# TensorE's increments on a drain behind each group of matmuls, in the three edge stages of a graph network

## The reference

```python
h = relu(layernorm(x))
x = x + L0(h, src, dst)                 # attention pooling, one logit per source node
h = relu(layernorm(x))
x = x + L1(h, edge_index, edge_attr)    # two TransformerConvs, 8 heads and 1 head

def L0(N, W1, w2, src, dst):
    e = (tanh(N @ W1.T) @ w2)[src]
    ex = exp(e - segment_max(e, dst)[dst])
    return segment_sum((ex / segment_sum(ex, dst)[dst])[:, None] * N[src], dst)

def transformer_conv(x, src, dst, edge_attr, ...):
    e = (edge_attr @ We).reshape(E, heads, C)
    alpha = sum(q[dst] * (k[src] + e), -1) / sqrt(C)
    p = exp(alpha - segment_max(alpha, dst)[dst])
    w = p / (segment_sum(p, dst)[dst] + 1e-16)
    agg = segment_sum((v[src] + e) * w, dst)
    return agg + (x @ Ws + bs)
```

## Time and profile before

| | us |
|---|---|
| time of the kernel, median of 3 runs | 9,990.61 |
| span of the profiled execution | 10,223.7 |
| TensorE busy, matmuls / weight loads | 6,865.3 (67%) / 5,286.7 (52%) |
| VectorE busy | 4,586.4 (45%) |
| ScalarE busy | 3,560.6 (35%) |
| GpSimd busy | 4,600.9 (45%) |
| pool stage, 213 to 3,200 | 2,987 |
| multi stage, 3,446 to 6,790 | 3,344 |
| single stage, 6,928 to 10,118 | 3,190 |

### The profile page before, as it was taken

One profiled execution on the slowest core, in us unless ns is written; L12 is line 12 of the kernel. 1 busy time (PEld: TensorE's weight loads), 2 busy tenths in 40 slices (PEclk: granted clock), 3 DMA queues, 4 the chain that ended last, 5 costly groups with the idle time before them and its releaser, 6 DMA issues. The chain is left out here.

```text
span 10223.7 us, 177251 instructions
## 1 busy us (share of the span) xinstructions
PE 6865.3 (67%) x40779; PEld 5286.7 (52%) x40779; DVE 4586.4 (45%) x12423; ACT 3560.6 (35%) x8557; POOL 4600.9 (45%) x4738
## 2 busy tenths in 40 slices
PE   3667666687655555555566666676777778778787
PEld 2556656576544345555555555553444444444445
DVE  3233333333346555566666666662333333333333
ACT  2233333333323344444444444442222323233332
POOL 2555544444441355544444444425544444444441
PEclk6666667767777677777777777787777878888888
DMA  2333333343322544444444444443333333333332
GB/s 77 95 102 103 101 102 105 105 109 107 94 59 80 151 136 137 136 138 138 135 136 136 137 137 141 136 141 74 76 75 76 77 74 76 74 75 75 73 75 62
DMA packets 1085568, 1056.97 MB, mean 103 GB/s; under 512 B 398824, under 2 KB 857244, under 8 KB 1084532
## 3 DMA queue, kind: packets, MB, share of 16 engines
q1 hardware_dynamic: 909364, 633.73, 22.8%
q0 software_dynamic: 175168, 411.90, 15.6%
HBM read 885.97 MB, written 159.07 MB: 102 GB/s over the span
## 5 line engine op out<-in xcount | busy, mean ns | idle before, releaser
L752 POOL DMA_INDIRECT ring_multi<-kv_rows,src_cols x1564 | 1606.5, 1027 | 1766.8 <-DVE kv L837 1205.8
L1133 POOL DMA_INDIRECT ring_single<-h_rows,src_cols x1564 | 1476.4, 944 | 1688.9 <-ACT row_single L1301 1180.6
L1133 POOL DMA_INDIRECT ring_pool<-pool_rows,src_cols x1564 | 1476.6, 944 | 1609.7 <-ACT row_pool L1301 1000.8
L1262 PE MATMUL ps_p_pool<-row_pool,probT_pool 128*128 128x129 f32 x3904 | 798.3, 369 | 998.8 <-DVE probT_pool L1226 924.9
L1262 PEld LDWEIGHTS ps_p_pool<-row_pool,probT_pool 128*128 128x128 f32 x3904 | 707.5, 271 | 1074.9 <-DVE probT_pool L1226 990.3
L1306 ACT ACTIVATE rowT<-ps_r 128x512 f32<-128x512 f32 x488 | 291.3, 597 | 2190.6 <-remote 1216.2
L1242 PE MATMUL ps_s_single<-rowT,cols 128*128 128x512 f32 x976 | 657.1, 762 | 465.2 <-issue 393.4
L1262 PE MATMUL ps_p_single<-row_single,probT_single 128*128 128x145 f32 x3904 | 737.9, 344 | 219.0 <-DVE probT_single L1226 181.0
L1213 DVE CUSTOM_DVE_ANT_0 masked_single<-mask_single,ps_s_single,start_single 128x512 f32<-128x512 bf16 x488 | 364.9, 748 | 986.4 <-PE ps_s_single L1244 524.7
L1262 PEld LDWEIGHTS ps_p_single<-row_single,probT_single 128*128 128x128 f32 x3904 | 663.5, 238 | 248.1 <-DVE probT_single L1226 202.8
L924 PE MATMUL ps_p_multi<-message_multi,onehot 128*128 128x136 f32 x3904 | 751.6, 354 | 4.8 <-issue 4.8
(11 more groups left out here) (224 smaller groups left out, 13519.3 us busy)
## 6 DMA issues: line engine op xcount, KB each, us to landing
term_multi<-edge_terms SPq DMA_DIRECT2D x488, 256.0 KB
edge_terms<-edge_term SPq DMA_DIRECT2D x391, 256.0 KB
dst_pool<-in_dst_rows SPq DMA_DIRECT2D x488, 128.0 KB
dst_multi<-in_dst_rows SPq DMA_DIRECT2D x488, 128.0 KB
dst_single<-in_dst_rows SPq DMA_DIRECT2D x488, 128.0 KB
query_multi<-query_parts SPq DMA_DIRECT2D x488, 96.0 KB
cols<-query_cols SPq DMA_DIRECT2D x488, 64.0 KB
ring_pool<-pool_rows,src_cols POOLq DMA_INDIRECT x1564
```

What stands on the lines that cost most here:

```text
L752: pool.indirect_dma_start(out=ring[:, u, j, :], out_offset=None, in_=rows, in_offset=bass.IndirectOffsetOnAxis(ap=g.src_cols[:, c:c + 1], ...
L1133: pool.indirect_dma_start(out=ring[:, u, j, :], out_offset=None, in_=rows, in_offset=bass.IndirectOffsetOnAxis(ap=g.src_cols[:, c:c + 1], ...
L1262: i = T_.matmul(ps_p[p3][:, 0:acc_w], probT[:, p3, j], row[:, u3, j, 0:acc_w], start=(j == 0), stop=(j == J - 1))
```

## The change

In the three edge stages no matmul or transpose of TensorE carries an increment any more. Behind each group stands a drain of TensorE (`pe.drain()`), and the drain carries the increment of the group, to the same semaphore and by the same amount. Groups, their order and the waits of every engine stay. The dense stages between are unchanged. From the diff, three of its thirteen places in full; the other ten have the same form:

```diff
                 if has(m2, ITEMS):
                     E["rows" if pool_k else "alpha"].wait(pe, m2)
                     E["scan"].wait(pe, m2 - 1)
-                    T_.transpose(ps_a[0:LOGITS, 0:P], alpha[:, u2].rearrange("p j h -> p (j h)"), g.ident[:]).then_inc(E["alphaT"].sem, 1)
+                    T_.transpose(ps_a[0:LOGITS, 0:P], alpha[:, u2].rearrange("p j h -> p (j h)"), g.ident[:])
+                    pe.drain().then_inc(E["alphaT"].sem, 1)
...
                     for j in range(J):
-                        i = T_.transpose(turned[:, j], onehotT[:, n % OB, j], g.ident_b[:])
-                    i.then_inc(E["onehotT"].sem, 1)
+                        T_.transpose(turned[:, j], onehotT[:, n % OB, j], g.ident_b[:])
+                    pe.drain().then_inc(E["onehotT"].sem, 1)
...
                     for j in range(J):
-                        i = T_.matmul(ps_e[n % 2][:, j * D:(j + 1) * D], attr[:, n % EB, j * P:(j + 1) * P], w_edge[:],
+                        T_.matmul(ps_e[n % 2][:, j * D:(j + 1) * D], attr[:, n % EB, j * P:(j + 1) * P], w_edge[:],
                                       start=True, stop=True)
-                    i.then_inc(term_made, 1)
+                    pe.drain().then_inc(term_made, 1)
```

More of the change, by code:

```diff
@@ L925, in step @@
                     E["scaled"].wait(pe, m5)
-                    T_.matmul(ps_p[:, 0:acc_w], g.ident[:], kept_sums[:, p5], start=False, stop=True)\
-                      .then_inc(E["partial"].sem, 1)
+                    T_.matmul(ps_p[:, 0:acc_w], g.ident[:], kept_sums[:, p5], start=False, stop=True)
+                    pe.drain().then_inc(E["partial"].sem, 1)
                 if has(m2, ITEMS):
@@ L938, in step @@
                     for j in range(J):
-                        i = T_.matmul(edge_max[:, j], onehotT[:, m3 % OB, j], fresh[:, p3], start=False, stop=(j == J - 1))
-                    i.then_inc(E["edge_max"].sem, 1)
+                        T_.matmul(edge_max[:, j], onehotT[:, m3 % OB, j], fresh[:, p3], start=False, stop=(j == J - 1))
+                    pe.drain().then_inc(E["edge_max"].sem, 1)
                 if has(n, ITEMS):
@@ L952, in step @@
                     for j in range(J):
-                        i = T_.matmul(tile_max[:, j], onehot[:, m2 % OB, j], ends[:, p2, j], start=True, stop=True)
-                    i.then_inc(E["tile_max"].sem, 1)
+                        T_.matmul(tile_max[:, j], onehot[:, m2 % OB, j], ends[:, p2, j], start=True, stop=True)
+                    pe.drain().then_inc(E["tile_max"].sem, 1)
                 if not pool_k and has(n, ITEMS):
@@ L961, in step @@
                         for k in range(3):
-                            i = T_.matmul(ps_q[:, j], onehotT[:, n % OB, j], query[:, u % QB, k, 0:D],
+                            T_.matmul(ps_q[:, j], onehotT[:, n % OB, j], query[:, u % QB, k, 0:D],
                                           start=(k == 0), stop=(k == 2))
                         for k in range(3 if single else 0):
-                            i = T_.matmul(tail_q[:, j], onehotT[:, n % OB, j], query[:, u % QB, k, D:ACC_W],
+                            T_.matmul(tail_q[:, j], onehotT[:, n % OB, j], query[:, u % QB, k, D:ACC_W],
                                           start=(k == 0), stop=(k == 2))
-                    i.then_inc(E["query"].sem, 1)
+                    pe.drain().then_inc(E["query"].sem, 1)
             rolled(pe, ITEMS, U, 5, step)
@@ L1243, in step @@
                         landed(pe, g.attrs_loaded, attrs_base, m1, u1, 32)
-                        T_.matmul(ps_s[p1][:], cols_tail[:, u1 % QB], edge_tail[:, u1], start=False, stop=True)\
-                          .then_inc(E["score"].sem, 1)
+                        T_.matmul(ps_s[p1][:], cols_tail[:, u1 % QB], edge_tail[:, u1], start=False, stop=True)
+                        pe.drain().then_inc(E["score"].sem, 1)
                     else:
@@ L1255, in step @@
                     for j in range(J):
-                        i = T_.transpose(ps_r[u % 2][:, j * P:(j + 1) * P], row[:, u, j, 0:D], g.ident[:])
-                    i.then_inc(E["rowT"].sem, 1)
+                        T_.transpose(ps_r[u % 2][:, j * P:(j + 1) * P], row[:, u, j, 0:D], g.ident[:])
+                    pe.drain().then_inc(E["rowT"].sem, 1)
                 if has(m3, ITEMS):
@@ L1261, in step @@
                     for j in range(J):
-                        i = T_.matmul(ps_p[p3][:, 0:acc_w], probT[:, p3, j], row[:, u3, j, 0:acc_w],
+                        T_.matmul(ps_p[p3][:, 0:acc_w], probT[:, p3, j], row[:, u3, j, 0:acc_w],
                                       start=(j == 0), stop=(j == J - 1))
-                    i.then_inc(E["partial"].sem, 1)
+                    pe.drain().then_inc(E["partial"].sem, 1)
                 if has(m2, ITEMS):
@@ L1268, in step @@
                     for j in range(J):
-                        i = T_.transpose(ps_t[p2][:, j * P:(j + 1) * P], prob[:, p2, j * P:(j + 1) * P], g.ident[:])
-                    i.then_inc(E["probT"].sem, 1)
+                        T_.transpose(ps_t[p2][:, j * P:(j + 1) * P], prob[:, p2, j * P:(j + 1) * P], g.ident[:])
+                    pe.drain().then_inc(E["probT"].sem, 1)
                 if not single and n < BLOCKS:
```

8 lines of the change are left out of this document (4 added, 4 removed).

## The result

The changed kernel takes 11,872.43 us (median of three runs, 11,853.55 to 11,911.47) for 9,990.61: 1.189 times as long, 95% interval 1.185 to 1.192. Its profiled execution has a span of 11,909.7 us for 10,223.7. Stages are compared by their spans in one profiled execution each. The one of before is 2.3% longer than its median here, so a stage of before looks up to that much too long beside a kernel whose runs of before took 9,963 to 9,980 us (e1 to e4, e9 and e10).

What follows compares the result with a forecast made beforehand. A chain of waits, with no engine full, was taken as the bound. The profiled 10,223.7 us plus 855 for pauses and 448 for holds gave 11,527, times 0.977 about 11,260 us timed; range 8,700 to 12,300.

Steps and rivals of the forecast that it cites:

- The pause: Behind each drain in the three edge stages TensorE loses 0.17 to 0.37 us, partly hidden by its waits: 855 us.
- The upper bounds of these two stages: The most that pauses behind drains could cost: 903 us in the multi stage and 625 in the single stage.
- I take no loss from pauses of 0.2 to 0.4 us: TensorE's clock in the edge stages loses nothing from pauses; some 390 us for longer holds in the range's upper part.
- The drain is held as the increment is: While gathers run, TensorE's drains come late and stop it, 1.0 us for each of 448 holds: +448 us.
- Rival A: Faster: a drain's increment isn't held by gathers, as another sender issues it; about 8,700 us with half the gain; chance 0.30.
- Rival C: Slower still: holds release one group of TensorE at a time, near 3.06 us lost per hold; 12,160 us timed; chance 0.15.
- Rival B: No change: all pauses fall into TensorE's idle time and running ahead in holds was of no use; 9,990 us; chance 0.05.
- The signs that I named: If right: pool steps 4.0 us, single 5.2, multi within 0.3 of 4.66, drains of several us, unshortened ScalarE "remote" waits.
- The sign against me: A reader (L1019 or L847) starting within 0.1 us of its group's end while gathers run would show the forecast wrong.

Runs made afterwards that it cites:

- e1: The changed kernel with its drains kept but the increments back on the last matmul of each group; 11,918 us, 1.193 times the kernel before.
- e4: The changed kernel with more TensorE work: multi's query group issued three times, pool's score and probT groups twice; 1.279 times the kernel before.
- e9: The kernel before, without drains; GpSimd waits for a block's last gather to land before issuing the next block's; ratio 0.999 to before.
- e10: The kernel before, without drains; GpSimd waits for landings behind each pair of gathers, the block's second and last; ratio 1.252 to before.
- e8: The changed kernel with plain DMAs for gathers, multi's query group issued three times, pool's score and probT groups twice; 0.951 times the kernel before.
- e3: The changed kernel with each gather replaced by a plain DMA of 128 consecutive rows; 9,892 us, 0.993 times the kernel before.
- e7: The kernel before, gathers kept, with drains on only some groups (partial and onehotT in multi, probT in pool and single); ratio 1.046 to before.
- e12: The kernel before, without drains; in all three stages GpSimd waits for a block's third gather to land before the next block; 9,065 us, ratio 0.890.
- e2: The kernel before with each gather replaced by a plain DMA of 128 consecutive rows; 6,368 us, ratio 0.638 to before.

## Why the prediction was right, and where not

The time lies in the range, and slower was the likeliest sign; but two of the three steps that carried it were wrong, and their errors lie on opposite sides: the drains without gathers cost 3,543 us for my 855, and the gathers cost 1,859 us less where I had 448 more. That the forecast of 11,260 came within 5% of 11,872 is in good part luck.

- *The pause.* The mechanism was right, the size too small. By rows I had 0.37 or 0.17 us a drain; from the modelled end it is 0.23 us each time, which against the old overlaps of 0.07 and 0.16 us is 0.30 to 0.39. The larger error was in what hides them: I took 57 and 76% of the steps and 0.20 us in multi, 855 us in all. Without gathers, pauses cost about 1.33 us a step in multi (e8, an estimate) and 1.64 in single (e3): 649 and 800 us for my 98 and 475. For pool, where no run with all of its drains stood at full clock, the price isn't separated from the clock. The upper bounds of these two stages, 903 and 625 us, were the better guide in sum, though single went over its own.
- *"I take no loss from pauses of 0.2 to 0.4 us"* is the step that failed most. The rows showed one pause ahead of one group; in the changed kernel they stand behind every group, and the multi stage ran at 1.2 GHz throughout. Of its 3.49 us a step without gathers, up to 2.16 are clock, 2.16 x 488 = 1,054 us for the multi stage alone; I had priced the clock at nothing, with 390 us in the range's upper part.
- *"The drain is held as the increment is", +448 us.* The premise holds: drains are held (L954 above, and e7), for 949 us in the changed kernel, which is more than I took. The sign of the term is wrong, because I counted the holds of before and took them to stay. They went: TensorE's idle time that comes with the gathers fell from 2,449 to 924 us, and long bursts of gathers went with it (2,074 gathers to 352). That shorter bursts mean fewer late announcements is shown without any drain by e9, e10 and e12, and by e7 from the other side. Why the bursts got shorter is argued, not shown: a TensorE that can't run ahead would free the ring's slots one at a time, and one that is merely slower would spread the gathers too. No run separates the two. In the multi stage shorter bursts don't explain all: they were mostly of four before, and TensorE's idle time with the gathers fell from 889 to 318 us there all the same; why is left open. That the gathers cost 2.75 us a step in e4 and 0.66 in the changed kernel is for the most part the clock (773 of 1,027 us), which had no further to fall in the changed kernel.
- *Rival A* described half of what happened: the late announcements did mostly go, but with the increments on the matmuls too (e1), so not by another sender, and the 3,543 us of pauses and clock outweighed it. The Trainium skill, "Perfetto Trace Analysis", section "Per-engine timelines", on which A leaned, names different senders for a matmul's and a drain's update; no run here shows a difference between the two.
- *Rival C* had a time (12,160 us) nearer to the result than my own, and the wrong reason: its loss was to come from holds let go one group at a time, but the holds became fewer, and the loss came from pauses and clock.
- *Rival B* is excluded by the time, and by e3: the packed steps of e2 became longer in each stage.
- The signs that I named: single steps of 5.2 us (5.58 without gathers), pool steps of 4.0 (5.35 at a clock of 0.71), multi within 0.3 us of 4.66 (wrong, 7.96), drains of several us in bursts (some: 270 of 7,223 end over 1 us late), "remote" waits as long as now (wrong: in the changed kernel a late increment shows as a late drain, 949 us in all, and in e1 659 us of "remote" waits are left). The sign against me, a reader that starts within 0.1 us of its group's end while gathers run, was there too (L1011).
- A reading that was off and changed nothing: GpSimd is busy for 46 to 49% of a stage, not 47 to 49 (single: 1,459.75 of 3,190).

## What to carry to other kernels

In these stages a drain behind each group cost TensorE more than its 0.23 us: it ended the overlap of weight loads with matmuls, and the pauses lowered the clock for a whole stage. Read the granted clock by stage before and after: the stage at 0.50 even got shorter by more work (3,886 to 3,482 us). When an engine's finished work is announced late, look for what else is going on at those moments and change that: here a single wait between blocks of gathers, of a length that lets announcements through (2.5 us from start to start, not 3.6), brought 11% where 7,223 drains cost 19%.

## What the runs showed of the hardware

While gathers follow each other at 1.25 us, TensorE's finished matmuls are announced late: waits that nothing else explains sum to 6,010 us in the kernel before and are absent with plain DMAs of as many rows (9,963 and 6,368 us; the difference also holds the gathers' slower pace, since plain DMAs start 0.53 us apart, and no run separates the two). A gap of some 2.5 us between the starts of two gathers lets about half of it through (e12), one of 3.6 us nearly all (e9). A drain behind matmuls is held as they are (e7). Without gathers a drain ends 0.02 us behind the modelled end of the last matmul, and the next matmul starts 0.21 us later (medians of e3; 0.31 behind onehotT).

What lowers the clock with the gathers is not shown; that it is lower with them is: 0.88 without and 0.73 with them in the multi stage of the kernel before.
